# RWKV layer: the divisor's inverse as exp(-ln u) on ScalarE with a Newton step in VectorE's products, and output and addition to X one batch later

## The reference

```python
x = _layernorm(x, ln_g, ln_b)
last_x = jnp.pad(x[:, :-1], ((0, 0), (1, 0), (0, 0)))
k = (x * time_mix_k + last_x * (1.0 - time_mix_k)) @ Wk.T      # v and r in the same way
td = jnp.exp(time_decay)
# per token t, from zero:  den = den * td + exp(k_t);  num = num * td + exp(k_t) * v_t
# wkv_t = num / (den + 1e-08)
out = jax.nn.sigmoid(r) * wkv @ Wo.T
```

## Time and profile before

| | |
|---|---|
| time, median of 3 runs | 1753.64 us (1750.28 to 1755.77) |
| profiled execution, first to last instruction | 1755.5 us |
| the same against the median | 1.9 us more |
| busy share: TensorE, VectorE, ScalarE, GpSimd | 83%, 77%, 58%, 61% |
| instructions | 38713 |
| mean granted TensorE clock | 0.881 |

### The profile page before, as it was taken

One profiled execution on the slowest core, in us unless ns is written; L12 is line 12 of the kernel. 1 busy time (PEld: TensorE's weight loads), 2 busy tenths in 40 slices (PEclk: granted clock), 3 DMA queues, 4 the chain that ended last, 5 costly groups with the idle time before them and its releaser, 6 DMA issues.

```text
span 1755.5 us, 38713 instructions
## 1 busy us (share of the span) xinstructions
PE 1451.3 (83%) x10263; PEld 1333.1 (76%) x10263; DVE 1352.7 (77%) x4027; ACT 1012.0 (58%) x2511; POOL 1075.3 (61%) x1700
## 2 busy tenths in 40 slices
PE   8799999688858999998527999775999972089996
PEld 8699999677746999998416999765988861079996
DVE  7789998799987888887655777674788885357775
ACT  4588888433316888884124666523777640056764
POOL 7438887777743354433664666631688877746665
PEclk9899999899977999997557999955989885589998
DMA  5111100930001111100312222031222201122210
GB/s 192 49 38 32 37 30 13 213 84 1 0 1 56 38 32 34 34 7 6 142 45 59 65 65 54 16 104 63 78 81 73 85 13 46 51 64 64 65 51 11
DMA packets 93267, 96.20 MB, mean 55 GB/s; under 512 B 12072, under 2 KB 75709, under 8 KB 92576
## 3 DMA queue, kind: packets, MB, share of 16 engines
q1 hardware_dynamic: 83168, 76.70, 15.2%
q0 software_dynamic: 9920, 17.35, 3.0%
HBM read 63.75 MB, written 33.78 MB: 56 GB/s over the span
## 4 chain that ended last, share of the span: by engine, by line
PE 62%; DVE 13%; issue 9%; POOL 8%; ACT 4%; DMA 1%; another core or an unknown queue 1%; DVEq 0%; SPq 0%; POOLq 0%; ACTq 0%
PE banks L593 5%; POOL rt_rows L867 4%; PE banks L582 4%; PE banks L1215 3%; PE banks L1202 3%; PE banks L573 3%; PE banks L574 3%; PE banks L575 3%; PE banks L1203 3%; PE banks L1204 3%; PE banks L1217 3%; PE banks L1216 3%; PE banks L1237 3%; PE banks L594 2%; PE banks L1187 2%
## 5 line engine op out<-in xcount | busy, mean ns | idle before, releaser
L1460 DVE TENSOR_TENSOR choice_hlo<-choice_h,choice_hhi 128x512 fp32r<-128x512 f32 x256 | 177.4, 733 | 23.1 <-ACT choice_hhi L1313 22.1
L1305 ACT ACTIVATE choice_h<-banks 128x512 f32<-128x512 f32 x256 | 152.6, 600 | 60.4 <-PE banks L1204 46.9
L826 DVE SCALAR_TENSOR_TENSOR top_h<-top_silu,top_xs,banks 128x176 f32<-128x176 f32 x364 | 128.5, 394 | 56.3 <-ACT top_silu L651 54.4
L867 POOL DMA_INDIRECT rt_rows<-X,top_slot x128 | 129.4, 1011 | 55.6 <-issue 37.3
L651 ACT ACTIVATE top_silu<-banks,top_xs 128x352 f32<-128x352 f32 x182 | 101.1, 555 | 87.9 <-PE banks L575 79.4
L1202 PE MATMUL banks<-choice_xin_hi,ec_w_hi 128*128 128x256 f32 x512 | 146.0, 285 | 4.8 <-ACT choice_xin_lo L1298 3.6
L1215 PE MATMUL banks<-choice_hhi,ec_w_hi 128*128 128x256 f32 x512 | 145.9, 285 | 2.7 <-DVE choice_hlo L1460 2.1
L1313 ACT ACTIVATE choice_hhi<-choice_h 128x512 fp32r<-128x512 f32 x256 | 146.6, 625 | 0.0
L1554 POOL TENSOR_SCALAR choice_y_hi_lo<-choice_yw 128x512 fp32r<-128x512 f32 x64 | 41.7, 652 | 167.3 <-ACT choice_yw L1328 166.2
L1203 PE MATMUL banks<-choice_xin_lo,ec_w_hi 128*128 128x256 f32 x512 | 144.0, 281 | 0.0
L1204 PE MATMUL banks<-choice_xin_hi,ec_w_lo 128*128 128x256 f32 x512 | 144.0, 281 | 0.0
(11 more groups left out here) (322 smaller groups left out, 5327.8 us busy)
## 6 DMA issues: line engine op xcount, KB each, us to landing
choice_token_row<-choice_tokens SPq DMA_DIRECT2D x64, 256.0 KB, 3.1
mlstm_run_row<-mlstm_run SPq DMA_DIRECT2D x32, 512.0 KB, 3.6
rt_rows<-rt_blank SPq DMA_DIRECT2D x2, 6188.0 KB, 36.8
top_xs<-rt_rows SPq DMA_DIRECT2D x182, 68.0 KB
X<-in_x SPq DMA_DIRECT2D x8, 512.0 KB, 6.8
ec_stage<-in_ec_w SPq DMA_DIRECT2D x2, 2048.0 KB
X<-rt_y SPq DMA_DIRECT2D x8, 512.0 KB, 6.9
rt_rows<-X,top_slot POOLq DMA_INDIRECT x128
```

The lines of the kernel that those rows point to most:

```text
L867: pool.indirect_dma_start(d.region[self.run], bass.IndirectOffsetOnAxis(ap=self.slot[:, t:t + 1], axis=0), self.sh.rows[:, t, :], None).th ...
L1460: dve.tensor_tensor(flat(self.hlo), self.h[:, c, :], flat(self.hhi).bitcast(F32), ALU.subtract).then_inc(self.hlo_done, 1)
```

## The change

The reciprocal is taken from VectorE. The divisor's second factor now has the other sign (er1 = -1 - exp(-r)), so that `under` is -u. ScalarE computes over = exp(-ln(u)) in two activations (`inverse`), in the step after that of the divisor, between exp(-r) of the batch and the copy for the next layer. VectorE corrects the value with one Newton step: it forms max(-u, -3e38) * over and num * over (`first_quotient`), and (the first + 2) * the second is `z` (`quotient`). Output product, addition to X, statistics and all that the next layer takes ahead move by one step (s - 1 to s - 2, s - 2 to s - 3, s - 3 to s - 4), and the pipeline has one step more. The activation tables' set is named ahead of the layer's first Exp. Apart from that, two semaphores are shared between layers, with a start value in the wait, and two that nobody waits for are gone.

```diff
--- before.py
+++ after.py
@@ -39,6 +39,7 @@
 EPS_HEAD = 1e-6
 CAPG = 15.0
 BIG = 1.0e30
+HUGE = 3.0e38
 ROUND = float(1 << 23)
 FB = 4
 XC = B // FB
...
@@ -1678,7 +1682,7 @@
 
     def steps(self, eng, step):
 
-        pipeline(eng, step, 1, B + 2, 6, B - 3)
+        pipeline(eng, step, 1, B + 3, 6, B - 3)
 
     def ahead_for_next(self, eng, part, b, u):
 
...
@@ -1712,8 +1716,8 @@
         def turn(b, u):
             pe.wait_ge(self.norm.done, b + 1)
             need(pe, self.x1_done, b)
-            if self.next is not None and inside(b - 4):
-                pe.wait_ge(self.next.xT_done, self.next.o + b - 3)
+            if self.next is not None and inside(b - 5):
+                pe.wait_ge(self.next.xT_done, self.next.o + b - 4)
             for t in range(TP):
                 i = pe.transpose(self.px[:, t * P:(t + 1) * P], self.norm.xn[:, u, t, :], ident[:, :])
             i.then_inc(self.xT_ready, 1)
@@ -1742,13 +1746,13 @@
                 turn(s + 1, 1 - u)
             if inside(s):
                 project(s, u)
-            if inside(s - 1):
-                out(s - 1, 1 - u)
+            if inside(s - 2):
+                out(s - 2, u)
             if self.next is not None:
-                if inside(s + 1) and inside(s - 2):
+                if inside(s + 1) and inside(s - 3):
                     pe.wait_ge(self.x1_done, s + 2)
-                self.ahead_for_next(pe, self.next.turn_first, s - 2, u)
-                self.ahead_for_next(pe, self.next.score, s - 3, 1 - u)
+                self.ahead_for_next(pe, self.next.turn_first, s - 3, 1 - u)
+                self.ahead_for_next(pe, self.next.score, s - 4, u)
 
         return turn, step
 
@@ -1757,6 +1761,7 @@
         x1, step = self.scalar_parts(act)
         if n == 0:
             act.wait_ge(self.w_in, 32)
+            act.preload_act_table_set("natural_log_exp_and_others")
             act.activation(self.td[:, :], self.cols[:, 0:1], ACT.Exp).then_inc(self.setup, 1)
         if n == 3:
             x1(0, 0)
@@ -1783,13 +1788,23 @@
             need(act, self.er1_done, b - 1)
             act.activation(self.er[:, u, :], self.pr[u][:, 0:T], ACT.Exp, scale=-1.0).then_inc(self.er_done, 1)
 
+        def inverse(b, u):
+
+            act.wait_ge(self.under_done, b + 1)
+            need(act, self.z_done, b - 1)
+            act.activation(self.over[:, u, :], self.under[:, u, :], ACT.Ln, scale=-1.0).then_inc(self.ln_done, 1)
+            act.wait_ge(self.ln_done, b + 1)
+            act.activation(self.over[:, u, :], self.over[:, u, :], ACT.Exp, scale=-1.0).then_inc(self.over_done, 1)
+
         def step(s, u):
             if inside(s + 1):
                 x1(s + 1, 1 - u)
             if inside(s):
                 exps(s, u)
+            if inside(s - 1):
+                inverse(s - 1, 1 - u)
             if self.next is not None:
-                self.ahead_for_next(act, self.next.first_xT, s - 2, u)
+                self.ahead_for_next(act, self.next.first_xT, s - 3, 1 - u)
 
         return x1, step
 
@@ -1810,28 +1825,34 @@
     def vector(self, dve):
         sh, X = self.sh, self.sh.X
 
-        def mix(b, u):
-            last = lambda part: part(dve, self.layer + 1, b - 1, 1 - u)
+        def scan_num(b, u):
             td = self.td[:, 0:1].to_broadcast([P, T])
             dve.wait_ge(self.ek_done, b + 1)
             dve.tensor_tensor(self.ekv[:, u, :], self.pkv[u][:, T:2 * T], self.ek[:, u, :], ALU.mult).then_inc(self.ekv_done, 1)
             dve.tensor_tensor_scan(self.den[:, u, :], td, self.ek[:, u, :], 0.0, ALU.mult, ALU.add)
             dve.wait_ge(self.ekv_done, b + 1)
             dve.tensor_tensor_scan(self.num[:, u, :], td, self.ekv[:, u, :], 0.0, ALU.mult, ALU.add).then_inc(self.scans_done, 1)
-            if inside(b - 1):
-                update(b - 1, 1 - u)
+
+        def divisor(b, u):
             dve.wait_ge(self.scans_done, b + 1)
             dve.wait_ge(self.er1_done, b + 1)
 
             dve.scalar_tensor_tensor(out=self.under[:, u, :], in0=self.den[:, u, :], scalar=1e-8, in1=self.er1[:, u, :],
                                      op0=ALU.add, op1=ALU.mult).then_inc(self.under_done, 1)
-            last(sh.moments.stats_of)
-            dve.wait_ge(self.under_done, b + 1)
-            dve.reciprocal(self.over[:, u, :], self.under[:, u, :]).then_inc(self.over_done, 1)
-            last(sh.moments.gather_of)
+
+        def first_quotient(b, u):
+
             dve.wait_ge(self.over_done, b + 1)
             need(dve, self.out_done, b - 1)
-            dve.tensor_tensor(self.z[:, u, :], self.num[:, u, :], self.over[:, u, :], ALU.mult).then_inc(self.z_done, 1)
+            dve.scalar_tensor_tensor(out=self.under[:, u, :], in0=self.under[:, u, :], scalar=-HUGE, in1=self.over[:, u, :],
+                                     op0=ALU.max, op1=ALU.mult).then_inc(self.first_done, 1)
+            dve.tensor_tensor(self.z[:, u, :], self.num[:, u, :], self.over[:, u, :], ALU.mult).then_inc(self.first_done, 1)
+
+        def quotient(b, u):
+
+            dve.wait_ge(self.first_done, 2 * b + 2)
+            dve.scalar_tensor_tensor(out=self.z[:, u, :], in0=self.under[:, u, :], scalar=2.0, in1=self.z[:, u, :],
+                                     op0=ALU.add, op1=ALU.mult).then_inc(self.z_done, 1)
 
         def update(b, u):
             dve.wait_ge(self.out_done, b + 1)
@@ -1840,10 +1861,16 @@
 
         def step(s, u):
             if inside(s):
-                mix(s, u)
-            if isinstance(s, int) and s == B:
-                update(s - 1, 1 - u)
-                sh.moments.moments_of(dve, self.layer + 1, s - 1, 1 - u)
+                scan_num(s, u)
+                divisor(s, u)
+            if inside(s - 1):
+                first_quotient(s - 1, 1 - u)
+            if inside(s - 2):
+                update(s - 2, u)
+            if inside(s - 1):
+                quotient(s - 1, 1 - u)
+            sh.moments.stats_of(dve, self.layer + 1, s - 2, u)
+            sh.moments.gather_of(dve, self.layer + 1, s - 2, u)
 
         step(0, 0)
         self.steps(dve, step)
@@ -1867,7 +1894,7 @@
         def er1(b, u):
             apart(pool, self.under_done, b - 1, self.sh.passed)
             apart(pool, self.er_done, b + 1, self.sh.passed)
-            pool.tensor_scalar(self.er1[:, u, :], self.er[:, u, :], 1.0, 1.0, ALU.mult, ALU.add).then_inc(self.er1_done, 1)
+            pool.tensor_scalar(self.er1[:, u, :], self.er[:, u, :], -1.0, -1.0, ALU.mult, ALU.add).then_inc(self.er1_done, 1)
 
         def norm(b, u):
             self.norm.gpsimd(pool, b, u, lambda: apart(pool, self.xT_ready, b - 1, self.sh.passed))
@@ -1883,7 +1910,7 @@
                 norm(s + 2, u)
             if inside(s):
                 er1(s, u)
-            self.scale_next(pool, s - 2, u)
+            self.scale_next(pool, s - 3, 1 - u)
 
         return norm, step
 
...
@@ -2132,7 +2160,7 @@
 
         def decay(b, u):
 
-            act.wait_ge(self.row_in[u], 8 * (b - u) + 16)
+            act.wait_ge(self.row_in[u], self.ROWS_BEFORE + 8 * (b - u) + 16)
             need(act, self.ct_done, NH * (b - 1))
             for h in range(NH):
                 n = NH * b + h
```

18 lines of the change are left out of this document (11 added, 7 removed).

## The result

The changed kernel takes 1747.05 us in the median (1741.39 to 1749.32, 4 runs), the kernel before 1753.89 (1750.28 to 1755.77, 4 runs). The ratio is 0.9945, 95% interval 0.9925 to 0.9965: about half a per cent faster, and the interval does not reach 1. The profiled execution has a span of 1747.3 us against 1755.5, so 8.2 less; 5.4 had been forecast.

A forecast was written before the change was run, and what follows sets the result against it. VectorE, without a gap, bounds the kernel at 4.94 us a batch, with TensorE and ScalarE's loop close at 4.58. 26 x (4.94 - 4.70) = -6.2, +0.5, +0.3 gives -5.4: 1748.0 us, range 1743.5 to 1757.

The forecast's parts named there:

- the beginning: Layer's start: Ln and Exp between batch 3's second exponential and batch 5's transpose lengthen 1.19 to 1.66 us, +0.47.
- the end: Layer's end: VectorE finishes the last batches' products and additions, and the layer ends a step later: +0.3 us (0 to 1).
- The ScalarE chain: Loop from transpose through second exponential, Ln, Exp and copy to next transpose: 4.70 us a batch, between 4.57 and 4.95.
- rival 3: ScalarE's Ln and Exp follow without delay, the loop stays at TensorE's 4.58 us a batch: 1744.5 us; chance 0.16.
- the 4.58 of the forecast: TensorE and ScalarE's loop before, without the wait for z: 4.58 us, so freeing VectorE gives at most 0.36 a batch.
- the 4.05 of the forecast: X is transposed 4.05 us after the batch's transpose, ScalarE is free 4.17 after it, so both chains nearly coincide.
- VectorE at 4.31, with 0.39 to spare: VectorE's new sum of instruction distances is 4.31 us a batch, 0.39 below the likeliest period of 4.70.
- Rival 1: GpSimd's norm products block VectorE's new products, up to 0.37 us each: slower, 1757 us, or 1767 with a third; chance 0.17.
- The sign to look for: In the profile after, VectorE is no longer full and waits some 0.3 us a batch for the first exponential.
- The table load: ScalarE's activation table load of 1.28 us stays a single one ahead of the layer, none in the loop: cost nothing.
- rival 4: ScalarE gets a table load for each Ln and Exp, 2 x 1.28 us a batch: +82 us; chance 1 in 100.

The follow-up runs named there:

- experiment 11: Changed kernel with VectorE's statistics and gathering kept apart and ScalarE's copy ahead of Ln and Exp, bank still shared: 4.30 us a batch, ratio 0.9922 to the kernel before.
- experiments 1 to 3: Changed kernel with the next layer's first transposes in another bank: 0.994 of before; without the Newton step: 0.9933; with both edits: 0.9848.
- the own bank: Changed kernel with the next layer's first transposes in the free half of r's banks, so transposes skip the copy wait: 4.61 us a batch, 0.994 of before.
- experiment 6: Changed kernel with Ln and Exp in the divisor's step, output and addition to X in the next, as before: 6.84 us a batch, 1.0291 of the kernel before.
- experiment 7: The changed kernel without the delay, with ScalarE's copy moved ahead of Ln and Exp: 4.85 us a batch, 0.9978 of the kernel before.

## Why the prediction was right, and where it was not

**Sign and size.** Forecast 1748.0, measured 1747.05. The forecast mechanism is what happened: the reciprocal left VectorE, z's wait vanished, and the loop through TensorE and ScalarE took over, the transposes waiting longer for the copy. That the two times are within 1 us is in part luck. The layer ends 8.8 us earlier where 5.4 were forecast; the period (2.3), the beginning (0.7) and the end (0.4) all missed to the same side. The medians differ by only 6.8, and executions of one kernel scatter by 5 to 8 us.

**The ScalarE chain** was forecast at 4.70 and measured 4.59 to 4.61. Er to Ln was 0.28 (taken 0.31), Ln to Exp 0.44 (0.46), Exp to copy 0.32 (0.33), copy to transpose 0.51 (0.53), and of the 0.03 for register instructions nothing shows. The wait of Exp for Ln was 0.03 beyond its end, near the 0.05 chosen between 0 and 0.18. Each link was a few hundredths too long, and with 26 batches this makes 2.3 us. The result lies between the forecast and rival 3, which had TensorE's 4.58; the copy stands right behind Exp, so the chain is not hidden, it is just short. (Rival 3's 1744.5 also counts nothing for the beginning.)

**TensorE's own loop is shorter than the 4.58 of the forecast.** The forecast took the wait for z out of the rows of before and was left with 3.01 us to the output product and 0.55 from there to the transposes of X. Without the wait these are 2.84 (424.57 to 427.41) and 0.45, together 0.27 less. So the copy could start 3.78 after the transposes (3.29 and the 0.49 of the forecast); ScalarE starts it at 4.08. The two chains are 0.3 apart and do not nearly coincide; the 4.05 of the forecast is the time at which the copy could start, not that at which X is transposed. Nor is 4.58 the least that is left when VectorE is freed: with the same shared bank experiment 11 takes 4.30. VectorE's measured 4.58 is another sum; nothing in the rows ties the two together.

**VectorE at 4.31, with 0.39 to spare: wrong.** This is the step that failed, and the time does not show it. It needs 4.58 (experiments 1 to 3). Of the 0.27 that was missing, 0.17 is the gathering: taken as 0.12 to the next product, it is 0.16 or about 0.42 (mean 0.29), since it now stands last in the step, where the "issue" time and a hand-over fall behind it. The last product (0.52 for 0.43), the second (0.39 for 0.34) and the first scan (0.64 for 0.60) lose 0.18 beside GpSimd; against that the other terms came out 0.08 lower, the second scan above all (0.79 for 0.82). The distance of 0.64 from statistics to gathering was in the sum and is right (0.63), but I took it for a given and did not ask what it would be worth to keep the two apart: 0.23 a batch. Had VectorE had the 0.39, the own bank would have gained by itself.

**Rival 1** was right in its mechanism: GpSimd's norm product and VectorE's last product meet, 0.85 for 0.43. One such meeting cost up to 0.43, more than the 0.37 that it was priced at, but only when VectorE's product starts with GpSimd's. In this layer, over all the kernels here, 281 of VectorE's products that started during a norm product took over 0.46 us, and every one of them ended 0.28 us after that norm product's end, however early it had started. So VectorE's product is held until GpSimd's is over. The Trainium skill, "SBUF — State Buffer", section "SBUF: two separate sides", has the port pair held for the whole instruction; the rows agree. The price stayed at 0.18 a batch, and with it VectorE came to 4.58 against 4.59, just under the point where it decides. That the time did not show VectorE's error is luck, and this is why neither of the two waits alone was worth anything.

**The sign to look for was misjudged.** I wrote that VectorE would wait for the first exponential some 0.3 a batch. These are all of its waits between 369 and 480 us, after:

```profile
DVE rwkv_ekv L1831 <- issue: 1.9, 11, 0.2
DVE moments L278 <- DVE bnstats L272: 1.5, 10, 0.2
```

None is for ScalarE, and the 6% in which it is idle is made of hand-overs. The version with its own bank, in which VectorE sets the pace, shows the same share of 100 us:

```profile
370.00:470.00 100.00, 90.40 (x526) 75.72 (x526) 94.27 (x263) 52.65 (x132) 77.70 (x132) 1.00 0.00 1
```

**The beginning** was forecast at +0.47 and came at -0.23. From the exponential of batch 3 to the transposes of batch 5 it is 2.18 us (forecast 1.66, before 1.19), but not because of Ln and Exp. The output product waited for z, the transposes of X stood behind it, and ScalarE, done with Exp, waited 0.52 for them before the copy:

```profile
362.87 0.71 PE L1740 MATMUL banks<-rwkv_w,rwkv_z 128*128 128x128 f32 x4 [0.73 <-DVE rwkv_z L1854]
...
363.84 0.38 ACT L1154 ACTIVATE choice_xT<-banks 128x256 f32<-128x256 f32 x1 [0.52 <-PE banks L1143]
```

Against that the exponential came 1.22 earlier. The first product of projection 3 in the changed kernel, and after it in the kernel before:

```profile
359.38 0.60 PE L1731 MATMUL banks<-rwkv_x,rwkv_w_now 128*128 128x256 f32 x2
```

```profile
358.92 1.00 PE L1727 MATMUL banks<-rwkv_x,rwkv_w_now 128*128 128x256 f32 x2
```

Its six pairs ran at 0.59 where four had run at 1.00 to 1.06; the slow stretch fell on projection 2, which had time. No experiment isolates this, and the column of batch 5 in the table scatters by 2 us between versions (363.35 to 365.38 in those with the delay, the last one aside), so a term of +0.47 could not have been told.

**The end** was forecast at +0.3 and is -0.1: from the transposes of batch 31 to the last addition it is 14.1 us, before 14.2.

**The table load, the Newton step, the delay.** One load, as forecast; without the naming line it would have been 136 us and not the 82 of rival 4, since TensorE's clock goes down as well. Without the delay, and with the copy queued behind Ln, the change would have been 2.9% slower (experiment 6); most of that is the copy's place, but with the copy first the version without the delay still keeps only 0.2% of the 0.55% (experiment 7).
